# Head-stacking transfers reordered, one transpose moved ahead in its step, and small vector work moved to GpSimd in an attention and experts kernel

## What is computed

```
kv = rmsnorm(xn @ W_kv) * g_kv          # 32 wide
qc = xn @ W_q                           # 64 wide
q  = [qc @ W_qdec , rope(qc @ W_qrope)] # 16 heads of 8 + 32
k  = [kv @ W_kdec , rope(xn @ W_krope)] # 16 heads of 8 + 32
v  = kv @ W_vdec                        # 16 heads of 8
attention = softmax(causal(q k^T / sqrt(40))) v @ W_o
experts   = top 2 of 8 (each: silu(xn W1 + b1) W2 + b2), weighted,
            + 0.1 * (silu(xn Ws1 + bs1) Ws2 + bs2)
```

## Time and profile before

| | us |
|---|---|
| median of 3 runs | 761.78 (761.53 to 764.14) |
| the profiled execution | 767.34 |
| its span | 765.6 |
| busy in the span: PE, DVE, ACT, POOL | 644.3, 588.3, 390.5, 300.1 |
| mean granted TensorE clock, share of full speed | 0.926 |

### The profile page before, as it was taken

How to read it: one execution, slowest core, us unless ns; L and a number is a source line. 1 busy time by engine, 2 the same in 40 slices (tenths; PEclk the granted TensorE clock), 3 DMA queues, 4 the chain that set the end, 5 groups by cost and what they waited for, 6 DMA issues and landing times.

```text
span 765.6 us, 14745 instructions
## 1 busy us (share of the span) xinstructions
PE 644.3 (84%) x4646; PEld 520.6 (68%) x4646; DVE 588.3 (77%) x1568; ACT 390.5 (51%) x842; POOL 300.1 (39%) x348
## 2 busy tenths in 40 slices
PE   0557978888887897888899888787889999999995
PEld 0445766667666776766777766665568888888884
DVE  3758889887788886869978878975647777779896
ACT  1212534554453463544545555443457777777772
POOL 3222542735546365464243343342300000357573
PEclk9957979999999998999999999978669999999998
DMA  4254656566565565655454554457714777889753
GB/s 123 85 178 153 192 182 195 158 216 208 178 202 183 192 199 183 204 175 204 138 152 152 167 166 159 137 158 233 235 55 152 247 249 249 259 292 297 237 170 91
DMA packets 66135, 141.66 MB, mean 185 GB/s; under 512 B 9054, under 2 KB 34699, under 8 KB 66059
## 3 DMA queue, kind: packets, MB, share of 16 engines
q1 hardware_dynamic: 61059, 131.41, 53.5%
...
...
## 4 chain that ended last, share of the span: by engine, by line
PE 49%; DVE 19%; DMA 12%; issue 10%; POOL 4%; SPq 3%; ACT 2%; POOLq 0%; ACTq 0%; DVEq 0%
PE bank L1668 8%; DMA QK<-mT 7%; PE bank L1686 5%; POOL QK L736 4%; PE bank L1416 3%; PE bank L1491 3%; PE bank L1432 3%; PE bank L1505 3%; DVE mx L1061 3%; PE bank L1418 3%; PE bank L1690 2%; SPq L489 2%; DMA QK<-heads_high 2%; PE bank L1508 2%; PE bank L1415 2%
## 5 line engine op out<-in xcount | busy, mean ns | idle before, releaser
L1061 DVE TENSOR_REDUCE mx<-bank 128x3 f32<-128x384 f32 x256 | 141.6, 554 | 78.5 <-PE bank L1508 76.1
L787 ACT ACTIVATE prob<-bank 128x384 f32<-128x384 f32 x256 | 125.5, 491 | 139.1 <-PE bank L1418 136.7
L660 POOL TENSOR_TENSOR rot<-rot,t 128x512 f32<-128x512 f32 x64 | 82.1, 1282 | 167.4 <-DVE t L1051 167.4
L1505 PE MATMUL bank<-QK 120*128 120x256 f32 x256 | 99.2, 388 | 32.8 <-issue 25.2
L736 POOL DMA_INDIRECT QK<-expert_outs,out_at x64 | 65.6, 1025 | 145.1 <-DMA expert_outs<-prob 126.8
L1359 DVE TENSOR_TENSOR QK<-vaug,QK 128x512 fp32r<-128x512 f32 x124 | 86.4, 698 | 41.1 <-ACT QK L881 38.5
L1416 PE MATMUL bank<-QK 122*128 122x256 f32 x256 | 90.9, 355 | 0.0
L1415 PE MATMUL bank<-QK 122*128 122x128 f32 x256 | 77.8, 304 | 11.5 <-DMA QK<-mT 11.5
L1491 PE MATMUL bank<-ident,rot 128*120 128x128 f32 x384 | 69.8, 296 | 14.8 <-DVE mx L1061 10.5
L1505 PEld LDWEIGHTS bank<-QK 120*128 120x128 f32 x256 | 55.7, 217 | 37.7 <-issue 28.0
L716 POOL DMA_INDIRECT expert_rows<-xn,place_of x64 | 66.2, 1034 | 34.0 <-PE bank L1418 23.9
(11 more groups left out here) (229 smaller groups left out, 1447.8 us busy)
## 6 DMA issues: line engine op xcount, KB each, us to landing
...
```

The costliest lines, as they stand in the source:

```text
L660: nc.gpsimd.tensor_tensor(r[n][:, 0:H, DC:D], r[n][:, 0:H, DC:D], t2[n][:, :, :], ALU.add).then_inc(s_rot, 1)
L787: act_f(prob[:, h % P_SLOTS, :], ST_PS[h % 2][:, P:4 * P], ACT.Exp, scale=SCALE).then_inc(s_exp, 1)
L1061: V.tensor_reduce(mx[:, 0:3, h], B_PS[bank_of(k)][:, 0:3 * P].rearrange("p (a c) -> p a c", a=3), AX.X, ALU.max).then_inc(s_bfree[bank_of( ...
L1505: mm(ps[:, 0:T], q[:, P:T], kk, start=True, stop=False, skip_group_check=True)
```

## The change

- In `restack`, the rows made of high parts come first for keys too (high, high, low). For group 0 the two high rows wait only for ACT's last high part (`s_hi`), and the wait for the freed bank stands right ahead of the low row.
- In `units_at`, ("n", half) comes ahead of ("t", order, half). Only step 3 has both.
- `normalised` moves from DVE at step 12 to POOL at step 3, right behind the -1/2 power (for batch 0 ahead of the presetting of `vaug`).
- The query stack (L1007, L1010) and `small_stacks` move from DVE to POOL, all at step 1: the query stack before the -1/2 power, kv's scaling and ks behind it. A cast becomes a multiplication by one.
- PE and ACT wait for the stacks by a semaphore that now counts two per batch. DVE's counted steps fall from 13 to 9.

```diff
@@ -34,7 +34,8 @@
 V_SLOTS, P_SLOTS = 3, 8
 SMW = RKV + RQ + E
 LN_EPS, RMS_EPS, TOP_EPS = 1e-5, 1e-6, 1e-9
-SMALL_STEPS = 13
+SMALL_STEPS = 9
+STACK_STEPS = 3
 INIT = 1 + 1 + 2
 
 
@@ -72,12 +73,12 @@
 def units_at(s):
 
     units = [(1, ("m", s - MAX_AT)) if s >= MAX_AT else (0, ("m", s - MAX_AT + H))]
+    if s in MROWS_AT:
+        ahead, half = MROWS_AT[s]
+        units.append((ahead, ("n", half)))
     if s in TURNED_AT:
         ahead, order, half = TURNED_AT[s]
         units.append((ahead, ("t", order, half)))
-    if s in MROWS_AT:
-        ahead, half = MROWS_AT[s]
-        units.append((ahead, ("n", half)))
     if s == TURN_STEP:
         units.append((-1, ("o",)))
     if s == WO_STEP:
@@ -333,6 +334,7 @@
         s_oT = sem("attention_normed")
         s_acc = sem("attention_added")
         c_a = sem("dve_small_steps")
+        c_p = sem("gpsimd_stack_steps")
         c_b = sem("dve_second_tile_maxima")
         c_n = sem("parted_max_high")
         c_c = sem("dve_sum_inverted")
@@ -480,12 +482,15 @@
             def restack(beta, side, i):
 
                 n, heads = "qk".index(side), HEADS_OF[i]
-                if i == 0:
-                    k = UNIT_NO[beta, ("t", 2 * n + 1, 1)]
-                    sp.wait_ge(s_bfree[bank_of(k)], FREE_NO[k])
+                k = UNIT_NO[beta, ("t", 2 * n + 1, 1)]
                 at_least(sp, s_st, (beta - 2) * H + heads[-1] + 1)
                 high, low = parts_of(beta, side)
-                for row, part in enumerate((high, high, low) if side == "q" else (high, low, high)):
+                rows_of = ((0, high), (1, high), (2, low)) if side == "q" else ((0, high), (2, high), (1, low))
+                for row, part in rows_of:
+                    if i == 0 and row == rows_of[0][0]:
+                        sp.wait_ge(s_hi, raw_no(beta, 2 * n + 1, 1) + 1)
+                    if i == 0 and row == rows_of[2][0]:
+                        sp.wait_ge(s_bfree[bank_of(k)], FREE_NO[k])
                     sp.dma_start(QK[row * D:(row + 1) * D, beta % 2, n, heads[0]:heads[-1] + 1, :].bitcast(F32),
                                  part[i * D:(i + 1) * D, 0:len(heads), :].bitcast(F32)).then_inc(stacked(beta, side)[0][i], 16)
 
@@ -645,6 +650,16 @@
             pool.wait_ge(s_pre, 5)
             pool.wait_ge(s_var, 1)
             nc.gpsimd.tensor_tensor(rstd[:, :], rstd[:, :], mhalf[:, :], ALU.pow).then_inc(s_rstd, 1)
+            def normalised(b):
+
+                at = slice(b * NT, (b + 1) * NT)
+                pool.wait_ge(s_rstd, b + 1)
+                at_least(pool, s_afill, 3 * b - 2)
+                for j in range(NT):
+                    nc.gpsimd.tensor_scalar(xn[:, b * NT + j:b * NT + j + 1, :], xres[:, b * NT + j:b * NT + j + 1, :],
+                                            mv[:, j, 0:1], rstd[:, j:j + 1], ALU.subtract, ALU.mult).then_inc(s_xn, 1)
+
+            normalised(0)
...
@@ -671,6 +686,29 @@
                 pool.wait_ge(c_n, done)
                 nc.gpsimd.tensor_tensor(nhl[:, half, :, 1, :], mx[:, 2:4, heads], nhl[:, half, :, 0, :],
                                         ALU.subtract).then_inc(s_nm, 1)
+
+            def stack_query(b, steps):
+
+                qc = smt[:, :, RKV:RKV + RQ]
+                pool.wait_ge(c_a, b * SMALL_STEPS + 7)
+                at_least(pool, s_afill, 3 * b)
+                steps.add(nc.gpsimd.tensor_tensor(qs[:, :, 0, :], qc, unit[:, 0:1].unsqueeze(1).to_broadcast([P, NT, RQ]),
+                                                  ALU.mult))
+                steps.need()
+                nc.gpsimd.tensor_tensor(qs[:, :, 1, :], qc, qs[:, :, 0, :], ALU.subtract).then_inc(s_small, 1)
+
+            def stack_keys(b, steps):
+
+                kv = smt[:, :, 0:RKV]
+                pool.wait_ge(s_rs, b + 1)
+                steps.add(nc.gpsimd.tensor_tensor(kv, kv, rs[:, :].unsqueeze(2).to_broadcast([P, NT, RKV]), ALU.mult))
+                steps.need()
+                steps.add(nc.gpsimd.tensor_tensor(ks[:, :, 0:3:2, :], kv.unsqueeze(2).to_broadcast([P, NT, 2, RKV]),
+                                                  unit[:, 0:1].unsqueeze(1).unsqueeze(1).to_broadcast([P, NT, 2, RKV]), ALU.mult))
+                steps.need()
+                nc.gpsimd.tensor_tensor(ks[:, :, 1, :], kv, ks[:, :, 0, :], ALU.subtract).then_inc(s_small, 1)
+
+            stacks = {b: Chain(pool, c_p, b, STACK_STEPS) for b in range(B)}
 
             def split_weights(e, part):
 
@@ -696,9 +734,13 @@
                     if known(b + 3) and b > -3 and s == NORM_STEP:
                         pool.wait_ge(s_var, b + 4)
                         nc.gpsimd.tensor_tensor(rstd[:, :], rstd[:, :], mhalf[:, :], ALU.pow).then_inc(s_rstd, 1)
+                    if known(b + 3) and b > -3 and s == NORM_STEP:
+                        normalised(b + 3)
                     if known(b + 2) and s == SUM_STEP:
+                        stack_query(b + 2, stacks[b + 2])
                         pool.wait_ge(s_ms, b + 3)
                         nc.gpsimd.tensor_tensor(rs[:, :], rs[:, :], mhalf[:, :], ALU.pow).then_inc(s_rs, 1)
+                        stack_keys(b + 2, stacks[b + 2])
                     if weights_at(b) is not None and s in SPLIT_AT:
                         split_weights(weights_at(b), SPLIT_AT[s])
 
@@ -831,7 +873,7 @@
                         act_f(xhl[:, (par + 1) % 2, 0, :], banks[0][:, 0:T], ACT.Copy).then_inc(s_xh, 1)
                     if known(b + 2) and s == SM_STEP:
                         sc.wait_ge(s_afill, (b + 2) * 3 + 2)
-                        at_least(sc, s_small, b + 2)
+                        at_least(sc, s_small, 2 * (b + 2))
                         act_f(smt[:, :, :], banks[1][:, :].rearrange("p (j c) -> p j c", j=NT)[:, :, 0:SMW],
                               ACT.Copy).then_inc(s_smh, 1)
                     if known(b + 2) and s == QK_STEP:
@@ -983,15 +1025,6 @@
                 steps.need()
                 V.tensor_scalar(rstd[:, :], mv[:, :, 1], LN_EPS, None, ALU.add).then_inc(s_var, 1)
 
-            def normalised(b):
-                i = b * NT
-                dve.wait_ge(s_rstd, b + 1)
-                at_least(dve, s_afill, 3 * b - 2)
-                for j in range(NT):
-                    at = slice(i + j, i + j + 1) if isinstance(b, int) else bass.ds(i + j, 1)
-                    V.tensor_scalar(xn[:, at, :], xres[:, at, :], mv[:, j, 0:1], rstd[:, j:j + 1],
-                                    ALU.subtract, ALU.mult).then_inc(s_xn, 1)
-
             def small_products(b, steps):
 
                 low = banks[1][:, :].rearrange("p (j c) -> p j c", j=NT)
@@ -1001,24 +1034,12 @@
                 steps.add(V.tensor_tensor(smt[:, :, 0:RKV + RQ], low[:, :, P:P + RKV + RQ],
                                           smt[:, :, 0:RKV + RQ], ALU.add))
                 steps.need()
-                kv, qc = smt[:, :, 0:RKV], smt[:, :, RKV:RKV + RQ]
+                kv = smt[:, :, 0:RKV]
                 steps.add(V.tensor_tensor(sq[:, :, :], kv, kv, ALU.mult))
-                at_least(dve, s_afill, 3 * b)
-                steps.add(V.tensor_copy(qs[:, :, 0, :], qc))
                 steps.need()
                 steps.add(V.tensor_reduce(ss[:, :], sq[:, :, :], AX.X, ALU.add))
-                steps.add(V.tensor_tensor(qs[:, :, 1, :], qc, qs[:, :, 0, :], ALU.subtract))
                 steps.need()
                 V.tensor_scalar(rs[:, :], ss[:, :], 1.0 / RKV, RMS_EPS, ALU.mult, ALU.add).then_inc(s_ms, 1)
-
-            def small_stacks(b, steps):
-                kv, qc = smt[:, :, 0:RKV], smt[:, :, RKV:RKV + RQ]
-                dve.wait_ge(s_rs, b + 1)
-                steps.add(V.tensor_tensor(kv, kv, rs[:, :].unsqueeze(2).to_broadcast([P, NT, RKV]), ALU.mult))
-                steps.need()
-                steps.add(V.tensor_copy(ks[:, :, 0:3:2, :], kv.unsqueeze(2).to_broadcast([P, NT, 2, RKV])))
-                steps.need()
-                V.tensor_tensor(ks[:, :, 1, :], kv, ks[:, :, 0, :], ALU.subtract).then_inc(s_small, 1)
 
             def rotate(beta, order, piece):
 
@@ -1309,19 +1330,15 @@
                     if known(b + 2):
                         if s == SUM_STEP:
                             small_products(b + 2, small[b + 2])
-                        if s == SMALL_STEP:
-                            small_stacks(b + 2, small[b + 2])
                             assert small[b + 2].n == SMALL_STEPS, small[b + 2].n
                     if known(b + 3):
                         if s == NORM_STEP:
                             normalise(b + 3, small[b + 3])
-                        if s == XN_STEP:
-                            normalised(b + 3)
                     if group_at(b) is not None and s in ROUTE_AT and ROUTE_AT[s] < len(ROUTE_AT) - 1:
                         router(group_at(b), ROUTE_AT[s])
                     if b == -3 and s == NORM_STEP:
                         split_small()
-                    if b == -3 and s == XN_STEP:
```

(3 more changed lines are left out.)

## The result

The changed kernel takes 751.81 us (median of four; 748.2 to 754.94), the kernel before 761.65 on the same chip in the same rounds (761.04 to 764.14). The ratio is 0.9876, 95% interval 0.9834 to 0.9917: faster by 9.8 us where 6 were forecast. The profiled execution took 754.94 us with a span of 752.8, that is 12.4 less than the profiled one of before (767.34).

A forecast was written before the change was run, and what follows sets the result against it. No single engine bounds it: PE is held at steps 3 and 9, SP's queue is behind in some turns. 3.1 - 0.4 + 0.6 + 0.6 + 0.3 + 2.6 = 6.8 us, 6 kept: 755.8 us; range 750.5 to 765.5.

The forecast's parts named there:

- more than summed: Rival: DVE, relieved of 1.7 us per turn, pulls maxima along and POOL's chain is no later; 751 us, chance 0.10.
- if the wait at step 9 stays: Sign of a wrong prediction: PE's idle before L1505, waiting for key group 0, remains instead of going or nearing 0.1 us.
- The other two signs: Signs of a wrong prediction: L1606 waits over 1 us for POOL's ks, or PE's clock falls in turns that had 1.00.
- free turns: Turns 0, 2, 6, 10 to 13, where SP's DMA queue isn't behind, so issuing group 0 earlier can gain.
- so each wait goes: Step 9 of turns 2, 6, 11, 12, 13: transfers 1.0 us earlier, PE 0.2 later; 4.09 - 1.0 = 3.1 us gained.
- Maxima first at step 3 ... I take nothing: Half 0's mT transfer starts some 1.3 us earlier, but PE waits for it in only a few turns; gain nothing.
- the 1.0 us that high rows first was to bring by itself: Key group 0 in free turns: low row issued at 415.15 instead of 416.13; gain 1.0 us, between 0 and 1.6.
- the order of the rows moves nothing: Rival: draining three 200 KB transfers sets group 0's landing, so only the DVE part stays; 760.3 us, chance 0.18.
- POOL's chain is long: Rival at L1606: POOL's new instructions cost 0.72 us each, making it 1.9 us late; up to 768.4 us, chance 0.12.
- router turn: One of four turns with a router, DVE busy 31.77 of 35.50 us; moving normalised rows gains 0.65 each, 2.6 in all.
- Queue-bound turns: Turns 1, 3, 4, 5, 7, 8, 9 up to step 9: SP is behind with expert weights; row order alone gains zero.
- The clock: Rival: changed idle at step 3 lowers PE's clock in free turns, 1.7 us each; 762 us, tail 767.6, chance 0.15.

The follow-up runs named there:

- the two traces of after: The changed kernel, unaltered, traced in the first comparison (0.9876 of before) and again on a chip of the later experiments (0.9867 of before).
- the two kernels with a hold: Changed kernel without maxima first, plus SP holding key group 0's first high row until ACT has copied the maxima (0.9857 of before) or their transfer has landed (1.0271).
- The kernel with SP's hold: Changed kernel without maxima first, plus SP holding key group 0's first high row until ACT has copied the maxima: 0.9857 of before.

## Why the prediction was right, and where it was wrong

The time, the sign and the range held, but the measured 751.8 us is nearer to the rival "more than summed" (751, given 0.10) than to the forecast, and the way there isn't the one forecast. By its own signs the prediction is half wrong: it was to be wrong "if the wait at step 9 stays", and that stayed, 24.9 us after 25.2. The other two signs came out for it: L1623 isn't late, and the free turns 2, 6 and 11 to 13 keep a clock of 1.00 behind step 3. That the sum still lands near is luck in part.

Two steps failed. One is "so each wait goes": the five waits at step 9 of turns 2, 6, 11, 12 and 13 sum to 2.7 and 2.8 us in the two traces of after where 4.09 was to go, and turns 0 and 10 have new ones of 1.2 and 0.9 us in sum. The other is "Maxima first at step 3 ... I take nothing", and with it the 1.0 us that high rows first was to bring by itself.

*High rows first.* As an order on SP it did what was worked out: alone it took the step 9 waits from 25.2 to 5.9 us. The step left out the engines behind the queues. It asked what the rows wait for, and not which transfer they would pass: the maxima's 16 KB come from ACT's queue and share the DMA engines with the rows. Passing them cost 19 us more of mT waits, as much as step 9 gave, and 9.0 us more of idle in the turns in all, and turned the forecast gain into a loss of 0.7%.

*Maxima first.* The size of the move was right: the mT issue comes 4.49 us after the turn's first small matmul (405.58 to 410.07) where it was 5.80 (408.01 to 413.81), 1.3 us earlier as forecast. The effect was taken from its own waits, and these hardly change (11.5 to 9.5 us, of which 5.3 and then 5.1 or 2.4 lie in the turns). Its worth is that it makes the first edit pay; that only shows when it is taken out: 1.8%.

*In the whole change* the sum came out near, but not from where it was booked. The free turns: four waits of 3.4 us less 0.2 each, less 0.4 for turns 0 and 10, makes 2.2 us for those in the table; they gave 3.0 and 4.7. Turn 2 gave nothing, turn 11 gave 0.2, and turn 0 is 1.0 us longer in one trace of after and 1.3 shorter in the other. The wait of step 9 didn't go. In turn 11 it is 0.47. The third row starts 7.44 us into the turn and was at 8.12, 0.7 us earlier rather than 1.0. The SP rows of after, turn 11:

```profile
411.44 1.53 SPq L494 DMA_DIRECT2D QK<-heads_high  x2
413.02 1.00 SPq L494 DMA_DIRECT2D QK<-heads_low  x1
```

The missing part is ACT's high part, which starts 5.29 us into the turn (410.87) and was at 4.61: 0.7 us later where 0.5 was taken. The landing stayed as far behind the last issue, 5.3 us against 5.2. So "the order of the rows moves nothing" was wrong, as they landed 0.5 us earlier in the turn. The distance stays at 5.1 to 5.5 us in the two kernels with a hold too; whether bytes set it or a fixed delay isn't shown.

About half of what the free turns gained in the first trace of after lies where the sum had nothing. These are the stretches of turn 10 and turn 12, from small transposes to small transposes, of before:

```profile
384.90:413.60 28.70, 26.57 (x228) 21.10 (x228) 22.63 (x69) 15.09 (x38) 11.40 (x14) 0.94 0.51 157
...
441.10:469.60 28.50, 24.89 (x229) 20.03 (x229) 23.01 (x69) 15.11 (x38) 12.53 (x16) 1.00 0.52 163
```

and of after:

```profile
383.80:411.10 27.30, 24.84 (x229) 19.98 (x229) 21.37 (x61) 15.01 (x38) 14.85 (x21) 1.00 0.51 165
...
438.40:465.10 26.70, 24.62 (x229) 20.10 (x229) 21.39 (x61) 14.99 (x38) 14.85 (x21) 1.00 0.52 168
```

Turn 10 had no wait at step 9, and was booked at a loss of 0.2. It gained 1.4 us, since the granted clock was 0.94 before and is 1.00. In before it fell right behind step 3, to a mean of 0.66 over the 5 us from 384.95 on, behind these three waits:

```profile
383.35 0.54 PE L1491 MATMUL bank<-ident,rot 128*120 128x128 f32 x3 [0.56 <-DVE mx L1061]
384.39 0.28 PE L1517 MATMUL bank<-ident,nhl 128*16 128x128 f32 x2 [0.50 <-DVE heads_low L1071]
384.95 0.37 PE L1606 MATMUL bank<-ident,qs 128*128 128x128 f32 x2 [0.28 <-DVE ks L1021]
```

Turn 11 has the same three within 0.01 us and kept 1.00. Such falls come in five of the turns 1 to 13 in before and in three and two of them in the two traces of after, at 1.7 us each. That may be a gain of the change, whose waits there are 0.31, 0.58 and 0.34 us, or chance: after without rows first has five, three of them where the first of the waits is 0.8 us. Over all executions the mean clock of after is 0.003 above that of before beside it, an estimated 2 of the 10 us, though six executions don't fix that to better than 2. Turn 12, which gained 1.8 us, lost a wait of 0.75 us for the maxima's second half.

*Small stacks on POOL* were sized well. POOL's rows of after in turn 11:

```profile
408.17 0.40 POOL L695 TENSOR_TENSOR qs<-smt,unit 128x128 fp32r<-128x128 f32 x1
408.65 0.46 POOL L698 TENSOR_TENSOR qs<-smt,qs 128x128 fp32r<-128x128 f32 x1
409.07 0.72 POOL L742 TENSOR_TENSOR rs<-rs,mhalf 128x2 f32<-128x2 f32 x1
409.87 0.29 POOL L704 TENSOR_TENSOR smt<-smt,rs 128x64 f32<-128x64 f32 x1
410.24 0.40 POOL L706 TENSOR_TENSOR ks<-smt,unit 128x128 fp32r<-128x128 f32 x1
410.72 0.32 POOL L709 TENSOR_TENSOR ks<-smt,ks 128x64 fp32r<-128x64 f32 x1
```

Forecast from a line between 16 and 512 elements were 0.41, 0.47, 0.30, 0.41 and 0.33; the chain takes 2.87 us (408.17 to 411.04) against 3.04. L1623 starts 3.12 us after DVE's smt addition ended (407.97), where before it was 3.24 and 3.4 had been forecast. The rival "POOL's chain is long" is out. The rule of the Trainium skill (SBUF — State Buffer, Who interferes with whom) on which DVE's L1038 could have been held for a POOL instruction isn't seen to bite: its median is 291 ns over 16 instructions, against 289 for the same one (L1005) before. In turn 11 of after GpSimd's L687 and L695 ran beside it, in before L672 did. The prediction says that what this rule gives is priced as a rival; no rival there is worked out from it.

*Normalised rows on POOL.* Priced at 0.4 to 0.5 us each; all 32 take 0.79 to 0.81:

```profile
L659 POOL TENSOR_SCALAR xn<-xres,mv,rstd x32: 786/798/806, 5.1 to 441.8; 128x128 f32<-128x128 f32 x32
```

The line was drawn through tensor_tensor instructions and was used for a tensor_scalar with two operands per partition. It cost nothing, as the slack was there. The gain was taken at 0.65 us in each router turn: three of them gave 1.4 us in one trace of after and 0.5 in the other, where 2.0 had been summed, so it is there at most in part. DVE is busy 30.87 us in turn 5 instead of 31.77.

*Queue-bound turns* were to keep their length. One by one they went from 30.7 to 31.9 and 30.5 (turn 4), and in sum by +1.7 and -1.1 us; the two traces of one kernel differ by more than the change. *The clock* rival had a true place and missed another. Behind step 3 the clock does fall in some turns, in before as in after, but in none of the free turns 2, 6 and 10 to 13 of after, so the loss that it feared isn't there. What it missed is the fall behind long waits, for the maxima at the first scores among them, which is an estimated half of the loss in after without maxima first.

What stays open: why rows first gives only 0.6% on top of the rest while maxima first gives 1.8%, where the two orders together give 1.0%; why the clock falls behind the same short waits in one turn and not in the next; how far stacks and normalised rows are worth anything; and how much of the first comparison's 12.4 us between profiles is the drain's clock by chance. The kernel with SP's hold had the shortest turns of all, 433.6 us against 437.2, but 0.9857 against 0.9867 can't be told apart.
